# Two of four x1 tiles on VectorE, made between its scalings, and a copy on ScalarE that adds an immediate one

## The chip, the core and the metric

The kernel runs on one core of a Trainium2 chip. The time is the device time of one execution in microseconds (us). Five engines work beside one another: TensorE (PE: matmuls and transposes), VectorE (DVE), ScalarE (ACT), GpSimd (POOL: tensor operations and the issue of indirect DMAs) and SyncE (SP: DMA queues). They meet at semaphores only: an engine runs its own instructions in order, and an instruction in front of which a wait stands holds all that stands behind it on that engine.

## What is computed

Two graph layers over 50,000 nodes of 128 features and 12,500 edges, with a residual and a layer norm after each. Cut to what matters here:

```
# layer 0 (gnn), N = 50000, 128 channels
pooled = relu(layer_norm(x[src] * (1 + coeff * w) @ pool_w + pool_b))   # per edge
agg    = max(segment_max(pooled, dst), 0)
h      = relu(layer_norm([x, agg] @ final_w + final_b))
x1     = (x + h - mean) / sqrt(var + eps)                                # no gain, no bias
# layer 1 (RGCN, 8 bases), its own residual and norm
out    = norm(x1 + [agg_b(x1), x1] @ weight + bias)
```

## The kernel before

Rows of x are taken in groups of 512 (`CH = 4` tiles of 128 rows). There are 98 dense groups (`DENSE`), which are treated as if no edge ended in them, and 25 edge groups, which compute the rows anew that do have edges and scatter them over the others. The 98 tiles of edges go through the same steps, one a step, from step 8 (`LATE`) on. A stage with indirect gathers and the eight basis matmuls follows.

The whole first part is one software pipeline. `step(s)` is written out on each engine, and its pieces work on groups of different age. For VectorE a step (L986) below `EDGE_ORDER` = 104 is, in this order:

- moments and spread of the row statistics (L994, L995, L1000), and between them L1029: h = max(h, 0) + x for four tiles at once, behind a wait for GpSimd's addition `pool_b`;
- `variances` (L1005), which waits for sums of squares that ScalarE makes (`act_h`, `act_y`, `act_e`: the last of these is L755, for the edge tile), `stats_of(0)` (L1017), `inverses` (L1050, reciprocal), `stats_of(1)`;
- `scanned` (L1060), the segment maximum of an edge tile as a scan;
- `means` (L1068), which waits for ScalarE's square root (`act_q`, L720);
- `scaled`: `pooled` of the edge tile (L1074, reads the bank HE, signals `dve_te`), then four scalings of H by rows and gain into `hn` (L1078), the last of which signals `dve_t`;
- `stats_of(2)`, `stats_of(3)`, `dense_out` (L1089), and `first_layer` (L1110): the tiles of x1 from `X1_ACT` = 3 on, so one tile, as scalar_tensor_tensor with a second tensor input that is one column of `st` broadcast over 128; it signals `dve_x`.

In steps from 104 on `stats_of` stands ahead, `scaled` and `first_layer` behind one another, then `dense_out`.

ScalarE in a dense step: `turned` (L712, x1T = VT + 1, four tiles at once, as an Identity activation whose bias is the column `one`), `roots` (L720, square roots), `rooted` (L704, four squares of Y), `first_layer` (L744, x1 tiles 0 to 2), `squares` (L704, four squares of H; L755, square of HE behind a wait for `pe_e`), `rows_turned` (L765, copy of 640 columns).

TensorE in a dense step: transposes of x1 (L513, behind `act_x` and `dve_x`), root matmuls (L524), transposes of x (L537), H (L549, L551); then it waits for `dve_te` of the same step, that is for L1074, and for the scan. Behind that wait stand L567 and L568 (the pooled tile of the step before, turned), L573 and L574 (HE of the next tile, signals `pe_e`), and all of the next step.

GpSimd in a dense step: L436 (adds beta to the four tiles of `hn`, behind `dve_t`, signals `pool_b`), two indirect gathers (L406, L413), and L427 (scales gathered rows by a column).

Of the kernel before, what the change touches and what calls it, by code (L numbers as in the profile page):

```python
# [16 lines left out]
P = 128  # L17
CH = 4
# [53 lines left out]
def gnn_kernel(nc, x, src_cols, dst_cols, dst_next_cols, dst_rows, dst_prev_rows, type_line,  # L72
# [34 lines left out]
    with ExitStack() as ctx:  # L107
# [121 lines left out]
        W_TOP, W_POOL, W_BOT, W_ROOT, W_BASE = 0, 1, 2, 3, 4  # L229
        GAM_F, BET_F, GAM_P, BET_P = 3, 4, 5, 6  # L230
        N_CONST = 9
        X1_ACT = CH - 1

        def tiles_in(q):

# [22 lines left out]
        def is_group(c, k):  # L258

            return 0 <= c - k < GROUPS  # L260

        def is_dense(c, k):
            return 0 <= c - k < DENSE
# [9 lines left out]
        def x1_tile(g, m):  # L273

            return x1[:, g % 2, m, :] if g < DENSE else agg_all[:, (g - DENSE) * CH + m, :]
# [397 lines left out]
        def _(act):  # L673
# [25 lines left out]
            def step(s):  # L699
# [8 lines left out]
                def turned():  # L708
                    if is_group(c, 5):
                        act.wait_ge(S["pe_c"], s - 4)  # L710
                        need(act, S["pe_d"], s - 6)
                        nc.scalar.activation(x1T[:, 1 - b, :, :].rearrange("p c d -> p (c d)"), VT, ACT.Identity,  # L712
                                             bias=one[:, 0:1]).then_inc(S["act_c"], 1)

                def roots():
                    if 2 <= c <= GROUPS + 3:
# [103 lines left out]
        def _(dve):  # L820
# [187 lines left out]
            def step(s):  # L1008
# [10 lines left out]
                if stats:  # L1019
# [2 lines left out]
                        dve.wait_ge(S["dve_m"], min(s - 4, GROUPS))  # L1022
                    first = moments(RES, TOP, 1 - b)
                    read_at = own.count
                if fresh:
                    if is_dense(c, 3):
                        dve.wait_ge(S["pool_b"], s - 2)
                    h = hn[:, (c - 3) % SLOTS, :, :].rearrange("p c d -> p (c d)")
                    dve.scalar_tensor_tensor(h, h, 0.0, rows[:, (c - 3) % SLOTS, 0:CH, :].rearrange("p c d -> p (c d)"),  # L1029
                                             ALU.max, ALU.add).then_inc(S["dve_v"], 1)  # L1030
                if stats:
                    own.need(first)
                    spread_at = spread(RES, TOP)
# [34 lines left out]
                        dve.scalar_tensor_tensor(st[:, 3, TOP:TOP + CH], power[:, 1 - b, 0, RES:TOP], -0.5, st[:, 7, RES:TOP],  # L1068
                                                 ALU.mult, ALU.mult).then_inc(S["dve_m"], 1)

                def scaled():
                    if is_tile(c, 2):
                        need(dve, S["pe_cp"], s - LATE - 3)
                        dve.scalar_tensor_tensor(pooled[:, b, :], HE, st[:, 7, EDG:EDG + 1],  # L1074
                                                 vec_raw[:, GAM_P, :], ALU.mult, ALU.mult).then_inc(S["dve_te"], 1)
                    if is_group(c, 2):
                        for m in range(CH):
                            last = dve.scalar_tensor_tensor(hn[:, (c - 2) % SLOTS, m, :], H[b][:, cols(m, m + 1)],  # L1078
                                                            st[:, 7, TOP + m:TOP + m + 1], vec_raw[:, GAM_F, :],
                                                            ALU.mult, ALU.mult)  # L1080
                            if m < CH - 1:
                                own.mark(last)
                        last.then_inc(S["dve_t"], 1)

                def dense_out():
                    if is_dense(c, 7):
# [13 lines left out]
                def first_layer():  # L1100
                    if is_group(c, 4):
                        dve.wait_ge(S["dve_m"], s - 3)
                        if is_dense(c, 4):
                            need(dve, S["pe_c"], s - 5)
                        else:
                            dve.wait_ge(S["pe_b"], s - 3)
                        if is_dense(c, 4) and is_dense(c, 6):
                            dve.wait_ge(x1_stored[b], 16 * since(c, 4 + b, 2))
                        for m in range(X1_ACT, CH):
                            last = dve.scalar_tensor_tensor(x1_tile(c - 4, m), hn[:, (c - 4) % SLOTS, m, :],  # L1110
                                                            st[:, 7, RES + m:RES + m + 1],
                                                            st[:, 3, TOP + m:TOP + m + 1].broadcast_to([P, D]),
                                                            ALU.mult, ALU.add)
                            if m < CH - 1:
                                own.mark(last)
                        last.then_inc(S["dve_x"], 1)
# [6 lines left out]
                if c < EDGE_ORDER:  # L1123
                    at = variances()
                    residual_ready()
                    stats_of(0)
                    inverses(at)
                    stats_of(1)
                    scanned()
                    means()  # L1130
                    scaled()
                    stats_of(2)
                    stats_of(3)
                    dense_out()
                    first_layer()
                    edge_beta_added()
                else:
                    residual_ready()
                    stats_of(0)
                    at = variances()  # L1140
                    stats_of(1)
                    inverses(at)
                    stats_of(2)
                    stats_of(3)
                    scanned()
                    means()
                    scaled()
                    first_layer()
                    dense_out()
                    edge_beta_added()  # L1150
# [125 lines left out]
```

## Time and profile before

| | us |
|---|---|
| median of 3 runs | 920.42 (920.28 to 921.27) |
| the profiled execution, its span | 1001.7 |
| steps in order of the dense loop with edge tiles | about 65 to 520 of the span |
| edge groups | about 520 to 700 |
| gathers and bases | about 700 to 1001.7 |

The profiled execution is 81.3 us longer than the median. In all rows, times are us, "mean ns" excepted, and the idle time in brackets at the end of a timeline row is that of the engine before the row, with what ended it. Instructions of one engine overlap a little: one can start while the one ahead is still written out. So what an instruction costs its engine is the distance to the start of the next, and not its duration.

### The profile page before, as it was taken

What the parts mean: (1) busy time and instruction counts of PE and PEld (TensorE: products, weight loads), DVE (VectorE), ACT (ScalarE), POOL (GpSimd) and SP (SyncE); (2) the same over time, 40 slices, a digit from 0 to 9 for tenths busy, and PEclk for the clock granted to TensorE, in tenths of its full rate; (3) what the DMA queues carried; (4) which work ended last, traced back from release to release, by engine and by line L of the source; (5) the groups of instructions that cost most, each with busy time, mean ns of one, the idle gap of its engine ahead of it and who ended that gap; (6) DMA issues with size and microseconds to landing.
All of it is one profiled execution on the core that took longest, in us unless ns stands there. A gap on an engine that the chain in (4) does not pass through costs nothing. (4 is left out here: it accounts for less than half of the span.)

```text
span 1001.7 us, 18559 instructions
## 1 busy us (share of the span) xinstructions
PE 821.0 (82%) x4588; PEld 589.6 (59%) x4588; DVE 802.6 (80%) x2823; ACT 622.5 (62%) x2862; POOL 662.4 (66%) x702
## 2 busy tenths in 40 slices
PE   5889999999999999999997777674687887888790
PEld 3677777777777777777786666463343433443340
DVE  6989999999999999999997677553377774776891
ACT  4799999999999999999996555555001111111121
POOL 2667777777777777777756646466756666667544
PEclk9899999999999999999999898987789898888895
DMA  4466575655655556556552122241466676666640
GB/s 114 127 220 216 189 224 196 202 196 192 203 193 192 191 193 202 201 199 202 199 183 88 63 61 69 72 187 41 139 246 238 234 242 229 209 217 249 204 157 28
DMA packets 88575, 175.46 MB, mean 175 GB/s; under 512 B 16715, under 2 KB 34023, under 8 KB 82198
## 3 DMA queue, kind: packets, MB, share of 16 engines
q1 hardware_dynamic: 71286, 144.02, 42.5%
q0 software_dynamic: 15744, 29.71, 9.9%
q8 instruction: 38, 0.62, 0.3%
q10 hardware_dynamic: 1440, 0.56, 0.2%
q14 instruction: 67, 0.55, 0.2%
HBM read 105.88 MB, written 70.88 MB: 176 GB/s over the span
## 5 line engine op out<-in xcount | busy, mean ns | idle before, releaser
L704 ACT ACTIVATE junk<-ps 128x128 bf16<-128x128 f32 x884 | 234.8, 295 | 48.0 <-remote 18.1
L656 PE MATMUL ps<-agg_all,w_cen 128*128 128x512 f32 (+1 forms) x400 | 197.0, 648 | 38.9 <-DVE agg_all L1177 26.4
L704 ACT ACTIVATION_READ_ACCUMULATOR junk<-ps 128x1 f32 x884 | 196.6, 227 | 0.0
L436 POOL TENSOR_TENSOR work<-work,vec_raw 128x512 f32<-128x512 f32 x98 | 124.4, 1269 | 87.0 <-DVE work L1078 86.3
L551 PE MATMUL ps<-w_cen,xT 128*128 128x128 f32 x984 | 164.2, 300 | 0.0
L656 PEld LDWEIGHTS ps<-agg_all,w_cen 128*128 128x128 f32 x400 | 82.1, 211 | 138.0 <-issue 137.7
L806 ACT ACTIVATE st<-st 128x4 f32<-128x4 f32 x25 | 5.1, 206 | 235.2 <-issue 122.3
L551 PEld LDWEIGHTS ps<-w_cen,xT 128*128 128x128 f32 x984 | 133.3, 201 | 29.9 <-issue 29.9
L406 POOL DMA_INDIRECT x_table<-agg_all,scat_i x98 | 102.3, 1044 | 73.2 <-ACT agg_all L744 32.2
L1177 DVE TENSOR_TENSOR agg_all<-coefs,ps 128x1024 f32<-128x1024 f32 x98 | 117.4, 1209 | 39.4 <-PE ps L642 19.6
L524 PE MATMUL ps<-w_cen,work 128*128 128x128 f32 x984 | 137.0, 284 | 2.0 <-ACT y_root L730 1.5
L1078 DVE SCALAR_TENSOR_TENSOR work<-ps,st,vec_raw 128x128 f32<-128x128 f32 x492 | 137.2, 340 | 0.4 <-ACT st L720 0.3
L413 POOL DMA_INDIRECT rows<-x_table,src_i x98 | 93.7, 956 | 59.6 <-issue 30.2
L524 PEld LDWEIGHTS ps<-w_cen,work 128*128 128x128 f32 x984 | 126.6, 201 | 2.9 <-issue 2.9
L406 POOL DMA_INDIRECT x_dst<-in_x,dst_i x98 | 105.7, 1078 | 31.9 <-DMA x_dst_table<-x_dst 21.1
L406 POOL DMA_INDIRECT out_rows<-work,scat_i x98 | 97.5, 995 | 43.6 <-issue 29.2
L744 ACT ACTIVATE work<-work,st 128x128 f32<-128x128 f32 x294 | 125.6, 516 | 0.6 <-DVE st L1068 0.6
L1017 DVE BATCH_NORM_STATS2 bn<-work 128x6 f32<-128x128 f32 x492 | 123.0, 271 | 0.9 <-issue 0.3
L413 POOL DMA_INDIRECT rows<-in_x,src_i x98 | 94.9, 968 | 30.0 <-issue 29.3
L537 PE MATMUL ps<-ident,rows 128*128 128x128 f32 x590 | 90.6, 285 | 29.3 <-ACT xT L765 17.0
L712 ACT ACTIVATE work<-ps,one 128x512 f32<-128x512 f32 x123 | 91.7, 745 | 10.4 <-remote 10.0
L513 PE MATMUL ps<-ident,work 128*128 128x128 f32 x392 | 63.0, 284 | 36.2 <-issue 27.6
(139 smaller groups left out, 1445.8 us busy)
## 6 DMA issues: line engine op xcount, KB each, us to landing
coefs<-coef_line SPq DMA_DIRECT2D x49, 1024.0 KB
rows<-in_x SPq DMA_DIRECT2D x97, 256.0 KB
x_table<-work SPq DMA_DIRECT2D x97, 256.0 KB
out_rows<-outb SPq DMA_DIRECT2D x97, 256.0 KB
x_dst_table<-x_dst SPq DMA_DIRECT2D x98, 64.0 KB
rows<-x_dst_table SPq DMA_DIRECT2D x24, 256.0 KB
same_prev<-mask_line SPq DMA_DIRECT2D x7, 224.0 KB, 4.2
x_dst<-in_x,dst_i POOLq DMA_INDIRECT x98
```

The costliest lines, as they stand in the source:

```text
L406: return pool.indirect_dma_start(*args, bounds_check=last_node, oob_is_err=False)
L413: return pool.indirect_dma_start(rows_of, None, table, by(columns, t))
L436: pool.tensor_tensor(h, h, vec_raw[:, BET_F:BET_F + 1, :].broadcast_to([P, CH, D]), ALU.add).then_inc(S["pool_b"], 1)
L524: last = pe.matmul(Y[b][:, cols(m, m + 1)], x1T[:, b, m, :], w_cen[:, W_ROOT, :], start=True, stop=True, skip_group_check=True)
L551: last = pe.matmul(H[1 - b][:, cols(m, m + 1)], xT[:, 1 - b, m, :], w_cen[:, W_TOP, :], start=False, stop=is_dense(c, 1), skip_group_check ...
L656: last = pe.matmul(MT[b][:, 0:n * D], w_cen[:, W_BASE + m, :], prod[:, b, m, 0:n, :].rearrange("p t d -> p (t d)"), start=(m == 0), stop=( ...
L704: last = nc.scalar.activation(junk[:, kind * CH + m, :], bank[:, cols(m, m + 1)], ACT.Square, accum_out=power[:, b, 1, TOP + kind * CH + m ...
L712: nc.scalar.activation(x1T[:, 1 - b, :, :].rearrange("p c d -> p (c d)"), VT, ACT.Identity, bias=one[:, 0:1]).then_inc(S["act_c"], 1)
L744: last = nc.scalar.activation(x1_tile(c - 4, m), hn[:, (c - 4) % SLOTS, m, :], ACT.Identity, bias=st[:, 3, TOP + m:TOP + m + 1], scale=st[ ...
L1017: own.mark(dve.bn_stats(bn[:, RES + m, :], hn[:, (c - 3) % SLOTS, m, :]))
L1078: last = dve.scalar_tensor_tensor(hn[:, (c - 2) % SLOTS, m, :], H[b][:, cols(m, m + 1)], st[:, 7, TOP + m:TOP + m + 1], vec_raw[:, GAM_F, ...
L1177: dve.tensor_tensor(prod[:, b, half, two, :], coefs[:, p % COEF_SLOTS, :, half, :].rearrange("p t m d -> p m t d"), GX[c % len(GX)][:, col ...
```

## The change

ScalarE makes x1 tiles 0 and 1 and no longer 2. VectorE makes tiles 2 and 3, by tensor_scalar with two columns of scalars in place of scalar_tensor_tensor with a broadcast column. In dense steps these two stand between the third and the fourth scaling. The scan goes ahead of the second statistics, and `pooled` of the edge tile goes from ahead of the scalings to behind `stats_of(2)`. L712 becomes an addition of the immediate 1.0, without the column. In edge steps the order stays, only tiles and operations change.

```
-        X1_ACT = CH - 1
+        X1_ACT = 2
...
-                        nc.scalar.activation(x1T[:, 1 - b, :, :].rearrange("p c d -> p (c d)"), VT, ACT.Identity,
-                                             bias=one[:, 0:1]).then_inc(S["act_c"], 1)
+                        nc.scalar.add(x1T[:, 1 - b, :, :].rearrange("p c d -> p (c d)"), VT, 1.0).then_inc(S["act_c"], 1)
...
-                def scaled():
+                def pooled_scaled():
                     if is_tile(c, 2):
                         need(dve, S["pe_cp"], s - LATE - 3)
                         dve.scalar_tensor_tensor(pooled[:, b, :], HE, st[:, 7, EDG:EDG + 1],
                                                  vec_raw[:, GAM_P, :], ALU.mult, ALU.mult).then_inc(S["dve_te"], 1)
+
+                def scaled(tiles=range(CH)):
                     if is_group(c, 2):
-                        for m in range(CH):
+                        for m in tiles:
...
-                            last = dve.scalar_tensor_tensor(x1_tile(c - 4, m), hn[:, (c - 4) % SLOTS, m, :],
-                                                            st[:, 7, RES + m:RES + m + 1],
-                                                            st[:, 3, TOP + m:TOP + m + 1].broadcast_to([P, D]),
-                                                            ALU.mult, ALU.add)
+                            last = dve.tensor_scalar(x1_tile(c - 4, m), hn[:, (c - 4) % SLOTS, m, :],
+                                                     st[:, 7, RES + m:RES + m + 1],
+                                                     st[:, 3, TOP + m:TOP + m + 1], ALU.mult, ALU.add)
...
                     inverses(at)
+                    scanned()
                     stats_of(1)
-                    scanned()
                     means()
-                    scaled()
+                    scaled(range(3))
+                    first_layer()
+                    scaled(range(3, CH))
                     stats_of(2)
+                    pooled_scaled()
                     stats_of(3)
                     dense_out()
-                    first_layer()
                     edge_beta_added()
```

## Rows read from the trace of the kernel before

**Rows 1.** Busy time by stretch (columns: PE, PEld, DVE, ACT, POOL, clock, DMA)
```profile
300.00:400.00 100.00, 91.97 (x631) 72.69 (x630) 95.34 (x376) 95.46 (x477) 73.50 (x79) 1.00 0.60 196
```
**Rows 2.** Timeline of VectorE over one dense step (start, duration, instruction)
```profile
344.56 0.68 DVE L1029 SCALAR_TENSOR_TENSOR work<-work,rows 128x512 f32<-128x512 f32 x1
...
346.43 0.14 DVE L1068 SCALAR_TENSOR_TENSOR st<-power,st 128x4 f32<-128x4 f32 x1
346.49 0.34 DVE L1074 SCALAR_TENSOR_TENSOR pooled<-ps,st,vec_raw 128x128 f32<-128x128 f32 x1
346.75 1.11 DVE L1078 SCALAR_TENSOR_TENSOR work<-ps,st,vec_raw 128x128 f32<-128x128 f32 x4
347.78 0.47 DVE L1017 BATCH_NORM_STATS2 bn<-work 128x6 f32<-128x128 f32 x2
348.18 0.67 DVE L1089 TENSOR_TENSOR outb<-ps,st 128x512 f32<-128x512 f32 x1
348.77 0.59 DVE L1110 SCALAR_TENSOR_TENSOR work<-work,st 128x128 f32<-128x128 f32 x1
349.28 0.15 DVE L994 TENSOR_TENSOR st<-bn 128x4 f32<-128x4 f32 x1
```
**Rows 3.** Timeline of all engines around another dense step
```profile
352.87 0.23 PE L567 MATMUL ps<-ones,edge_beta 3*128 3x128 bf16 x1
352.88 1.27 POOL L436 TENSOR_TENSOR work<-work,vec_raw 128x512 f32<-128x512 f32 x1 [0.74 <-DVE work L1078]
...
353.60 0.49 PE L574 MATMUL ps<-w_cen,xT 128*128 128x128 f32 x2
...
353.71 0.59 DVE L1110 SCALAR_TENSOR_TENSOR work<-work,st 128x128 f32<-128x128 f32 x1
...
354.47 1.49 POOL L406 DMA_INDIRECT x_dst<-in_x,dst_i  x1 [0.32 <-DMA x_dst_table<-x_dst]
...
357.27 0.41 POOL L427 TENSOR_TENSOR rows<-rows,e_scale 128x128 f32<-128x128 f32 x1
```
**Rows 4.** L1110 by itself, dense (100 to 500) and edge steps (560 to 620)
```profile
L1110 DVE SCALAR_TENSOR_TENSOR work<-work,st x80: 584/593/1240, 101.1 to 498.3; 128x128 f32<-128x128 f32 x80
```
```profile
L1110 DVE SCALAR_TENSOR_TENSOR agg_all<-work,st x9: 341/341/344, 561.2 to 617.3; 128x128 f32<-128x128 f32 x9
```
**Rows 5.** Timeline of ScalarE, from one release by TensorE to its next step
```profile
336.50 0.28 ACT L704 ACTIVATE junk<-ps 128x128 bf16<-128x128 f32 x1 [1.02 <-PE ps L524]
```
```profile
341.22 0.30 ACT L704 ACTIVATE junk<-ps 128x128 bf16<-128x128 f32 x1
```
**Rows 6.** Timeline of ScalarE, from the square of HE to the next copies
```profile
56.78 0.36 ACT L755 ACTIVATE junk<-ps 128x128 bf16<-128x128 f32 x1
...
57.03 0.79 ACT L765 COPY xT<-ps 128x640 f32<-128x640 f32 x1
...
57.60 0.80 ACT L712 ACTIVATE work<-ps,one 128x512 f32<-128x512 f32 x1
```
**Rows 7.** Timeline of an edge step where each engine waits for the one before
```profile
544.08 0.59 ACT L730 COPY y_root<-ps 128x512 f32<-128x512 f32 x1 [1.97 <-remote]
544.56 0.22 ACT L720 ACTIVATE st<-st 128x13 f32<-128x13 f32 x1
544.81 0.17 DVE L1068 SCALAR_TENSOR_TENSOR st<-power,st 128x4 f32<-128x4 f32 x1 [1.96 <-ACT st L720]
544.89 0.35 DVE L1074 SCALAR_TENSOR_TENSOR pooled<-ps,st,vec_raw 128x128 f32<-128x128 f32 x1
...
545.29 0.09 PEld L567 LDWEIGHTS ps<-ones,edge_beta 3*128 3x128 bf16 x1 [2.65 <-DVE pooled L1074]
```
**Rows 8.** Timeline: a tensor_scalar of VectorE within an indirect DMA's issue
```profile
585.01 0.98 POOL L406 DMA_INDIRECT x_table<-agg_all,scat_i  x1 [5.98 <-ACT agg_all L744]
...
585.36 0.23 DVE L929 TENSOR_SCALAR agg_now<-agg_now 98x128 f32<-98x128 f32 x1
...
586.29 0.98 POOL L406 DMA_INDIRECT x_table<-agg_all,scat_i  x1 [0.30 <-issue]
```

More of the change, by code:

```diff
@@ L1024, in step, with residual @@
                     read_at = own.count
[L1025 to L1030, printed above, removed]
+                def residual():
+                    if fresh:
+                        if is_dense(c, 3):
+                            dve.wait_ge(S["pool_b"], s - 2)
+                        h = hn[:, (c - 3) % SLOTS, :, :].rearrange("p c d -> p (c d)")
+                        dve.scalar_tensor_tensor(h, h, 0.0,
+                                                 rows[:, (c - 3) % SLOTS, 0:CH, :].rearrange("p c d -> p (c d)"),
+                                                 ALU.max, ALU.add).then_inc(S["dve_v"], 1)
+                residual()
                 if stats:
@@ L1082, in scaled @@
                                 own.mark(last)
-                        last.then_inc(S["dve_t"], 1)
+                            else:
+                                last.then_inc(S["dve_t"], 1)
                 def dense_out():
@@ L1146, in step @@
                     means()
+                    pooled_scaled()
                     scaled()
```

## The prediction

> **What bounds the kernel now.** I read the busy time by stretch first, which finds the long even part and its clock, then the timelines of one step, engine by engine, and last the same instruction in two stretches. In the dense stretch TensorE, VectorE and ScalarE are busy for 92, 95 and 95 of 100 us, at full granted clock [rows 1]. No engine has room by itself, so the order within a step decides. L1110 stands once in each dense step, 80 times from 101.1 to 498.3 [rows 4], so a step takes 397.2 / 79 = 5.03 us on average. An undisturbed one takes 353.71 - 348.77 = 4.94 [rows 2, 3]: in it VectorE starts one instruction close behind the other from L1029 to L994, and no wait for a semaphore shows [rows 2]. The rest, 0.09 a step, are stalls of ScalarE of up to a microsecond (rows 5, the first, is one), which reach VectorE later.
>
> One instruction of VectorE is longer than its work. L1110 takes 0.59 in dense steps and 0.34 in edge steps [rows 4]. In the dense step it runs while GpSimd adds beta: L436 ends at 352.88 + 1.27 = 354.15 and L1110 at 354.30 [rows 3]. In edge steps there is no L436. So some 0.25 us of each dense step is VectorE held by GpSimd. Without it VectorE's step would be 4.69. ScalarE by itself needs 341.22 - 336.50 = 4.72 for a step that it goes through without a long wait [rows 5]. These are the two near ties of today.
>
> **The change, part by part.**
>
> *L1110 goes from the end of the step.* It holds VectorE for 349.28 - 348.77 = 0.51 [rows 2]. That is removed.
>
> *Two tensor_scalar come in.* The trace has none of this form with two columns of scalars. Nearest is L929, 98x128 with immediates, 0.23 long [rows 8]; instructions of that length give way to the next some 0.08 early, as L1074 does (0.34 long, next start after 0.26 [rows 2]), so 0.15. The statistics L1017, one input and no scalar column, give way after (348.18 - 347.78) / 2 = 0.20; the scalings L1078, with one scalar column, after (347.78 - 346.75) / 4 = 0.26 [rows 2]. So a scalar column costs about 0.06 (an estimate, as L1078 also has a second tensor). The bounds for one tensor_scalar, called t, are 0.15 (the columns are free) and 0.20 + 2 x 0.06 = 0.32. L929 with one or two columns gives 0.21 or 0.27. I take t = 0.22, nearest to L929 with one column paid in full, and two of them 0.44. VectorE's own step is then 4.94 - 0.51 + 0.44 = 4.87, 0.07 less than now.
>
> L929 is the one row of this operation, and it is shorter than L1017 though it has a similar size. The Trainium skill, VectorE: DVE Perf Modes, "Mode 2×_2P", says that a one-input fp32 operation from SBUF to SBUF moves two elements a cycle; it agrees with L929. By its table of costs (58 cycles and one for two elements at 0.96 GHz) t would be an estimated 0.13, and VectorE's step 4.69.
>
> *ScalarE loses one of three L744 and the bias column.* A tile of L744 holds it for at least the 57.03 - 56.78 = 0.25 that the square of one tile takes [rows 6]; L712 to L720 becomes what a copy of the same size without a column takes, 544.56 - 544.08 = 0.48 [rows 7], a tenth less. ScalarE's own step falls from 4.72 to 4.37 or less. It is no bound any more, and part of the 0.09 a step from its stalls should be absorbed; I leave 0.05 (an estimate: half).
>
> *`pooled` (L1074) is moved behind three scalings, two x1 tiles, a fourth scaling and one statistics.* This is the part that costs. TensorE waits for it in the same step, ahead of L567, and L567, L568, L573, L574 and the whole next step are queued behind that wait. Now L1074 ends 0.40 after L1068 starts [rows 2], and L567 shows no idle time ahead of it [rows 3]: nobody waits. After the change it ends 0.06 + 3 x 0.26 + 2t + 0.26 + 0.20 + 0.34 = 1.63 + 2t after L1068 starts [rows 2]. A closed loop of one step hangs on it: L1074, then TensorE 0.05 later (544.89 + 0.35 to 545.29 [rows 7]), L567 to the end of L574 in 354.09 - 352.87 = 1.22 [rows 3], ScalarE another 0.05 later (an estimate, as the last hop), L755 0.25, L765 0.57 [rows 6], L712 0.48 [rows 7], then L720, to L1068 of the next step 0.25 [rows 7]. ScalarE's order allows nothing else: L720 stands behind L765 and L712. Sum: 1.63 + 0.05 + 1.22 + 0.05 + 0.25 + 0.57 + 0.48 + 0.25 = 4.50, plus 2t = 4.94. Today the same loop has 0.40 in place of 1.63 + 2t and some 0.10 more for L712: 3.4, with 1.5 us to spare. All of that is spent.
>
> *The fourth scaling is later, so GpSimd's L436 is.* It starts 0.08 behind the scaling's end, at 1.17 + 2t + 0.08 after L1068, ends at 2.52 + 2t, then L1029 may go, and from L1029 to L1068 it is 346.43 - 344.56 = 1.87 [rows 2]: 4.39 + 2t, some 0.05 more for the hop: 4.88. Just below the loop above.
>
> *The scan ahead of the second statistics:* the same two instructions stand between L1050 and L1068, nothing. *TensorE* gets x1 earlier, but with 92 of 100 us busy [rows 1] its own step is about 4.6: nothing either way. *Edge steps* (25): VectorE has one tile more (2t - 0.26 = 0.18), ScalarE one less; both tiles are needed, and GpSimd issues a scatter every 586.29 - 585.01 = 1.28 [rows 8], four to a group, 5.1 a step, which hides that. If that cover went, 25 x 0.18 = 4.5 us. Behind 700 nothing is changed.
>
> **Sum.** The longest of the loops is 4.94, with 0.05 for stalls 4.99, against 5.03. About 90 dense steps have all parts (455 us from 65 to 520, by 5.03): 90 x -0.04 = -3.6 us in the profiled execution, from 1001.7 to 998.1. That execution is 81.3 longer than the median, and where isn't shown; I take the same difference: 920.4 - 3.6 = 916.8.
>
> **The rivals.**
>
> *Cheap tiles.* If t is 0.15, the loop is 4.80 and the average 4.85: -0.18 x 90 = -16, 904. For it: L929. Against: two scalar columns, of which none is seen to be free. With the 0.13 of the Trainium skill, VectorE: DVE Perf Modes, it would be an estimated 901.
>
> *GpSimd gets in the way of the x1 tiles (slower).* L1110 shows that VectorE is held when it reads through what GpSimd holds. The two tensor_scalar stand from 0.83 to 1.27 after L1068. In rows 3 L427 starts 357.27 - 352.88 = 4.39 after L436, behind a gather that was late and long (L406, 1.49). With that distance it would start at 1.69 + 4.39 - 4.94 = 1.14 after L1068, on the second tile. L1029 will now start right behind L436 and so ahead of L406, and may make L406 long each time. If L427 falls on the tiles in most steps, they wait up to its 0.41, and this lies on the loop in full. It decides from the point where L427 starts later than 0.42 after L1068, 0.41 ahead of the tiles. A mean of 0.2 a step, with t = 0.22 to 0.27, with the 0.05 of stalls gives 5.19 to 5.29, and +14 to +23: 935 to 944. Against: GpSimd is idle for 0.74 ahead of L436 [rows 3], and the tiles stand in that gap in a step where it is punctual.
>
> *The tile isn't cheaper than today's.* If t is 0.26, what L1078 takes, the loop is 5.02 and the average 5.07: +3.6, 924.
>
> *Issue of the DMAs suffers.* In edge steps a tensor_scalar would fall into scatters. The rows speak against it: L929 ran inside one, which took 0.98 like the next [rows 8]. If each of 50 held the queue for its 0.22, that is +11 on the forecast: 928. The Trainium skill, SBUF — State Buffer, "Who interferes with whom", has this rule: VectorE in a two-port mode and GpSimd shut each other out, writing of descriptors included; by it the time would be the same 928, in edge steps, and the trace doesn't agree for L929.
>
> **How the numbers follow.** Forecast 0.41 (911 to 923, of which faster 0.23, same 0.12, slower 0.06), cheap tiles 0.22 (901 to 911), GpSimd in the way 0.23 (926 to 944), tile not cheaper 0.09 (same 0.03, slower 0.06), DMA issue 0.05. Faster by over 0.2% 0.45, within 0.2% (about what a measurement of this kernel can tell) 0.15, slower 0.40. The range, 902 to 939, leaves out the ends of the first and second rival.
>
> **What would show it.** Right: in dense steps TensorE's load for L567 idle, released by L1074; VectorE's L1068 idle, released by L720, which starts at once behind L712; ScalarE idle ahead of L755; steps of 4.9 to 5.0. L1110's 0.59 gone. Wrong: tensor_scalar rows of 0.4 and more that end with a GpSimd row; no wait at L567; L1029 waiting for L436 by more than 0.1; a changed pace between 520 and 700. The number is wrong by 1.8 us for each 0.01 in t.

## The result, and the profile after

| | kernel before | changed kernel |
|---|---|---|
| device time, median | 920.85 us | 940.75 us (940.13 to 941.15) |
| ratio | 1 | 1.0207, 95% interval 1.0186 to 1.0228 |
| span of a profiled execution | 916.4 us | 939.2 us |

The change makes the kernel 2.1% slower. Forecast was 916.8, in a range of 902 to 939.

Executions come in two kinds: beside some runs the kernel before takes about 920 us, beside others 985 to 1003, called the 920 kind and the 1000 kind from here on. The profile behind the prediction (span 1001.7) is of the second kind. The profile of before in the table above is another execution (`before_3` below), of the first kind, like the profile of the changed kernel. So all comparisons of totals below are made within one kind. Whether the kind belongs to the chip isn't shown: runs of both kinds carry chip number 0.

First, the busy time by stretch, as in [rows 1] (PE, PEld, DVE, ACT, POOL, clock, DMA). The changed kernel:

```profile
300.00:400.00 100.00, 87.04 (x622) 71.15 (x623) 96.19 (x388) 85.19 (x441) 81.41 (x78) 1.00 0.58 192
```

The kernel before, in an execution of the same kind (before_3):

```profile
300.00:400.00 100.00, 93.70 (x650) 74.83 (x649) 97.24 (x385) 98.73 (x491) 75.30 (x82) 1.00 0.60 199
```

The granted clock is 1.00 in both, the upper of its two levels. TensorE and ScalarE are busy for 7 and 14 us less in 100 (ScalarE also has one x1 tile less to make in each step). The list of waits of the changed kernel from 100 to 500 (us in total, times, longest) names for whom they wait:

```profile
PEld ps L567 <- DVE pooled L1078: 67.6, 77, 1.3
ACT junk L754 <- PE ps L574: 58.7, 77, 1.0
PE ps L567 <- DVE pooled L1078: 53.1, 77, 1.1
POOL work L436 <- DVE work L1084: 39.0, 77, 1.0
```

Once in each of 77 steps TensorE waits 0.88 us for the moved `pooled` (now L1078; lines behind the change are shifted, L1068 is L1072 and L755 is L754), and ScalarE waits 0.76 for TensorE. Those are two of the links of the prediction's closed loop. Its rows, from one step of the timeline of all engines:

```profile
353.89 0.16 DVE L1072 SCALAR_TENSOR_TENSOR st<-power,st 128x4 f32<-128x4 f32 x1
...
353.97 0.86 DVE L1084 SCALAR_TENSOR_TENSOR work<-ps,st,vec_raw 128x128 f32<-128x128 f32 x3
...
354.75 0.68 DVE L1117 TENSOR_SCALAR work<-work,st 128x128 f32<-128x128 f32 x2
354.82 0.51 POOL L427 TENSOR_TENSOR rows<-rows,e_scale 128x128 f32<-128x128 f32 x1
355.35 0.34 DVE L1084 SCALAR_TENSOR_TENSOR work<-ps,st,vec_raw 128x128 f32<-128x128 f32 x1
...
355.61 0.28 DVE L1016 BATCH_NORM_STATS2 bn<-work 128x6 f32<-128x128 f32 x1
...
355.76 1.26 POOL L436 TENSOR_TENSOR work<-work,vec_raw 128x512 f32<-128x512 f32 x1 [0.43 <-DVE work L1084]
355.81 0.33 DVE L1078 SCALAR_TENSOR_TENSOR pooled<-ps,st,vec_raw 128x128 f32<-128x128 f32 x1
...
356.19 0.09 PEld L567 LDWEIGHTS ps<-ones,edge_beta 3*128 3x128 bf16 x1 [0.83 <-DVE pooled L1078]
...
356.92 0.49 PE L574 MATMUL ps<-w_cen,xT 128*128 128x128 f32 x2
...
357.06 0.69 DVE L1030 SCALAR_TENSOR_TENSOR work<-work,rows 128x512 f32<-128x512 f32 x1
...
357.17 1.49 POOL L406 DMA_INDIRECT x_dst<-in_x,dst_i  x1
...
357.45 0.28 ACT L754 ACTIVATE junk<-ps 128x128 bf16<-128x128 f32 x1 [0.72 <-PE ps L574]
...
357.71 0.69 ACT L764 COPY xT<-ps 128x640 f32<-128x640 f32 x1
...
358.29 0.61 ACT L712 ACTIVATE work<-ps 128x512 f32<-128x512 f32 x1
...
358.78 0.22 ACT L719 ACTIVATE st<-st 128x13 f32<-128x13 f32 x1
...
359.03 0.17 DVE L1072 SCALAR_TENSOR_TENSOR st<-power,st 128x4 f32<-128x4 f32 x1
```

From start to start along the loop: L1072 0.08, three scalings 0.78, two tiles 0.60, fourth scaling 0.26, statistics 0.20, then 355.81 to 356.19 for L1078 and the hop, 1.26 to the release of L754 at 357.45, then 0.26, 0.58, 0.49 and 0.25. Sum 5.14, which is 359.03 - 353.89, and the median step of this kernel. The last link, from ScalarE's root L719 to VectorE's L1072, makes a wait too short for the list: L719 ends at 359.00 and L1072 starts at 359.03, and in the median L1072 comes 0.25 behind the start of the statistics ahead of it, where it comes 0.18 behind when the root is early (wait_moved below). The same rows in the kernel before, L1068 to L1068 of VectorE:

```profile
302.82 0.14 DVE L1068 SCALAR_TENSOR_TENSOR st<-power,st 128x4 f32<-128x4 f32 x1
...
307.72 0.14 DVE L1068 SCALAR_TENSOR_TENSOR st<-power,st 128x4 f32<-128x4 f32 x1
```

4.90. A step is read from here on as the distance between two of these instructions. Where the time of the whole went is a sum over three stretches, in us. The dense stretch goes from the start of this instruction in step 10 to its start in step 104; the edge stretch follows, and then the rest:

| kernel | kind | median step, 100 to 500 | mean of 94 steps | dense | edge | rest | span |
|---|---|---|---|---|---|---|---|
| before, first profile | 1000 | 4.92 | 5.055 | 475.1 | 157.1 | 310.9 | 1001.7 |
| before_3 | 920 | 4.91 | 4.958 | 466.0 | 122.5 | 271.0 | 916.4 |
| changed | 920 | 5.14 | 5.211 | 489.8 | 119.4 | 271.5 | 939.2 |

Of the 22.8 us between the two spans on the 920 kind, the dense steps take +23.8, the edge stretch -3.1, the rest and the start +0.5 and +1.6. The two kinds have the same median step for the kernel before; they differ in single long steps, and above all in the edge stretch and behind it. Median steps are therefore compared across kinds below, totals aren't.

### The profile page after: what moved, and what is told of

The parts are those of the page before. It is cut to its first block and busy times, and to the rows that moved or that the text cites. A ratio compares the mean times of both kernels' runs of the same rounds, so it can differ in the third digit from the quotient of the medians.

```text
span 939.2 us, 18559 instructions
## 1 busy us (share of the span) xinstructions
PE 769.8 (82%) x4588; PEld 566.3 (60%) x4588; DVE 824.2 (88%) x2946; ACT 569.3 (61%) x2739; POOL 706.3 (75%) x702
## 5 line engine op out<-in xcount | busy, mean ns | idle before, releaser
L656 PE MATMUL ps<-agg_all,w_cen 128*128 128x512 f32 (+1 forms) x400 | 177.7, 598 | 2.0 <-DVE agg_all L1186 1.2
L436 POOL TENSOR_TENSOR work<-work,vec_raw 128x512 f32<-128x512 f32 x98 | 124.0, 1265 | 71.6 <-DVE work L1084 71.3
L406 POOL DMA_INDIRECT x_dst<-in_x,dst_i x98 | 143.9, 1469 | 15.7 <-DMA x_dst_table<-x_dst 1.7
L1084 DVE SCALAR_TENSOR_TENSOR work<-ps,st,vec_raw 128x128 f32<-128x128 f32 x492 | 145.8, 342 | 0.4 <-ACT st L719 0.3
L1016 DVE BATCH_NORM_STATS2 bn<-work 128x6 f32<-128x128 f32 x492 | 133.9, 277 | 0.9 <-DVE st L1004 0.3
L524 PE MATMUL ps<-w_cen,work 128*128 128x128 f32 x984 | 132.0, 278 | 0.5 <-DVE outb L1096 0.5
L406 POOL DMA_INDIRECT x_table<-agg_all,scat_i x98 | 101.2, 1033 | 40.2 <-issue 26.6
L656 PEld LDWEIGHTS ps<-agg_all,w_cen 128*128 128x128 f32 x400 | 76.2, 196 | 87.3 <-issue 86.9
L524 PEld LDWEIGHTS ps<-w_cen,work 128*128 128x128 f32 x984 | 121.5, 194 | 1.0 <-issue 1.0
L406 POOL DMA_INDIRECT out_rows<-work,scat_i x98 | 97.4, 994 | 29.8 <-issue 28.6
L413 POOL DMA_INDIRECT rows<-in_x,src_i x98 | 95.0, 969 | 29.9 <-issue 29.6
L413 POOL DMA_INDIRECT rows<-x_table,src_i x98 | 93.5, 954 | 31.8 <-issue 28.6
L743 ACT ACTIVATE work<-work,st 128x128 f32<-128x128 f32 x196 | 89.1, 527 | 0.6 <-DVE st L1072 0.6
L1030 DVE SCALAR_TENSOR_TENSOR work<-work,rows 128x512 f32<-128x512 f32 x123 | 84.9, 690 | 0.0
L537 PEld LDWEIGHTS ps<-ident,rows 128*128 128x128 f32 x590 | 69.9, 145 | 22.9 <-ACT xT L764 11.8
```

Source lines behind the costliest of these rows:

```text
L406: return pool.indirect_dma_start(*args, bounds_check=last_node, oob_is_err=False)
L413: return pool.indirect_dma_start(rows_of, None, table, by(columns, t))
L436: pool.tensor_tensor(h, h, vec_raw[:, BET_F:BET_F + 1, :].broadcast_to([P, CH, D]), ALU.add).then_inc(S["pool_b"], 1)
L524: last = pe.matmul(Y[b][:, cols(m, m + 1)], x1T[:, b, m, :], w_cen[:, W_ROOT, :], start=True, stop=True, skip_group_check=True)
L537: last = pe.transpose(XT[:, cols(m, m + 1)], rows[:, slot, m, :], ident[:, :])
L656: last = pe.matmul(MT[b][:, 0:n * D], w_cen[:, W_BASE + m, :], prod[:, b, m, 0:n, :].rearrange("p t d -> p (t d)"), start=(m == 0), stop=( ...
```

## The experiments

Each ratio is to the kernel before timed beside it, so within one kind. Line numbers are those of the run's own kernel.

**pooled_first: the changed kernel with `pooled` ahead of the scalings again.** This takes the loop through L1078 away and leaves the tiles.

```diff
                     means()
+                    pooled_scaled()
                     scaled(range(3))
                     first_layer()
                     scaled(range(3, CH))
                     stats_of(2)
-                    pooled_scaled()
                     stats_of(3)
```

> The changed kernel, with pooled of the edge tile back ahead of the scalings; all else as changed. Theory A (two loops of a step: one by TensorE, ScalarE and back to VectorE through pooled, 5.14 us; one by GpSimd's beta addition, from the fourth scaling over L436 to the residual L1030, 5.03): the first falls to under 4.2, but the fourth scaling comes 0.26 later, so the second rises to 5.2 or 5.3: 944 to 956, slower than the change, with no wait of TensorE for pooled and a wait of VectorE ahead of L1030. Theory B (only the wait of TensorE for pooled costs): VectorE's own work decides, 4.94 to 5.03 a step, 921 to 931. Theory C (the tensor_scalars or the meeting with L427 cost, wherever pooled stands): as the change, 938 to 943.

953.24 against 921.54, ratio 1.0329 (1.0306 to 1.0353); median step 5.29. Timeline of that kernel, GpSimd and VectorE:

```profile
303.51 1.27 POOL L436 TENSOR_TENSOR work<-work,vec_raw 128x512 f32<-128x512 f32 x1 [0.69 <-DVE work L1084]
...
304.34 0.46 DVE L993 TENSOR_TENSOR st<-bn 128x4 f32<-128x4 f32 x1
...
304.81 0.69 DVE L1030 SCALAR_TENSOR_TENSOR work<-work,rows 128x512 f32<-128x512 f32 x1
```

L436 ends at 304.78 and L1030 starts at 304.81. The second loop of the prediction (fourth scaling, L436, L1030 and back) now carries the step: with `pooled` back in front it is some 0.25 longer (5.29, against 5.04 below). The place of `pooled` was right. Two loops lie close together, and shortening one is worth only the distance to the next.

**wait_moved: the changed kernel, TensorE waits for `pooled` only ahead of L573 and L574.** In the code HE (written by L573 and L574) and the output of L567 and L568 lie in one bank of PSUM, so a wait for ScalarE's read of HE stands ahead of L567 in this kernel, and `pooled` waits for L568 of its own step.

```diff
                 if is_tile(c, 2):
-                    pe.wait_ge(S["dve_te"], s - LATE - 1)
...
                     pe.wait_ge(S["dve_te"], s - LATE - 2)
+                    pe.wait_ge(S["act_e"], min(s - LATE - 1, TILES))
...
+                if is_tile(c, 2):
+                    pe.wait_ge(S["dve_te"], s - LATE - 1)
                 if is_tile(c, 1):
                     if c == LATE + 1:
...
-                        need(dve, S["pe_cp"], s - LATE - 3)
+                        need(dve, S["pe_cp"], s - LATE - 2)
```

> The changed kernel, where TensorE does L567 and L568 (pooled of the step before, turned) ahead of its wait for pooled of this step; the wait stands in front of L573. pooled waits for L568, and L567 for ScalarE's last square, since they share a bank. Theory A: the first loop loses the 0.58 of L567 and L568; the next longest are TensorE's own chain with pooled in it, 4.99, and GpSimd's, 5.03: 928 to 934. Theory B: VectorE's own work, 4.94 to 5.03, 921 to 931. Theory C: unchanged, 938 to 943.

937.24 against 921.54, ratio 1.0163 (1.0144 to 1.0182), above the 928 to 934 expected; median step 5.04. Timeline (L573 is now L574):

```profile
302.07 1.26 POOL L436 TENSOR_TENSOR work<-work,vec_raw 128x512 f32<-128x512 f32 x1 [0.43 <-DVE work L1085]
...
302.50 0.09 PEld L574 LDWEIGHTS ps<-pool_bias,ones 3*128 3x128 bf16 x1 [0.69 <-DVE pooled L1079]
...
303.37 0.69 DVE L1031 SCALAR_TENSOR_TENSOR work<-work,rows 128x512 f32<-128x512 f32 x1
...
304.84 0.21 ACT L720 ACTIVATE st<-st 128x13 f32<-128x13 f32 x1 [0.21 <-DVE st L1055]
```

The loop through `pooled` is open now: ScalarE stands idle for 0.21 ahead of its root L720 and waits for VectorE, which in the changed kernel it doesn't. The median step became 5.14 - 5.04 = 0.10 shorter, the 94 dense steps 9.8 us, and they stop at GpSimd's loop: L1031 starts 0.04 after L436 ends. The total improved less, as the edge stretch took 126.4 in place of 119.4; why wasn't tried. So with the loop through `pooled` opened, the changed kernel is still slower than before.

**pooled_late and one_tile: half of the change each.** pooled_late is the kernel before with `pooled` moved behind `scaled` and `stats_of(2)`, with all its tiles as they were:

```diff
                     means()
                     scaled()
                     stats_of(2)
+                    pooled_scaled()
                     stats_of(3)
                     dense_out()
                     first_layer()
```

one_tile is the changed kernel with three tiles on ScalarE:

```diff
-        X1_ACT = 2
+        X1_ACT = 3
```

> The kernel before, with one edit alone: in dense steps pooled of the edge tile goes behind the four scalings and the third statistics. Theory A: the loop through pooled is 4.61 without x1 tiles in it, under the others; the last scaling comes 0.26 earlier, L436 too, and L1110 isn't held any more (0.34 in place of 0.59), so VectorE needs 4.69 and ScalarE 4.72 a step: 900 to 905. Theory B (pooled behind the scalings costs by itself): 921 or more. If the hold of L1110 is hidden anyway: 919 to 922.

> The changed kernel with X1_ACT = 3: ScalarE makes three x1 tiles as before, VectorE one, by tensor_scalar between the third and the fourth scaling. Theory A: both loops lose a tile of 0.26 to 0.30: 4.84 to 4.88 and 4.73; ScalarE's own step 4.62: 911 to 917. If ScalarE with three tiles is the bound (it was near it before): 920 or more. If the tile isn't on the path: unchanged, 938 to 943.

pooled_late: 906.72 against 921.54, ratio 0.9823 (0.9789 to 0.9857), step 4.74. one_tile: 911.87, ratio 0.9893 (0.9877 to 0.991), step 4.80. Both are faster than before. pooled_late was expected at 900 to 905 and misses that by 1.7. The window of pooled_late, and rows of its VectorE and GpSimd:

```profile
300.00:400.00 100.00, 96.76 (x679) 78.00 (x678) 96.94 (x403) 100.00 (x507) 77.48 (x85) 1.00 0.63 209
```

```profile
301.33 0.16 DVE L1068 SCALAR_TENSOR_TENSOR st<-power,st 128x4 f32<-128x4 f32 x1
...
302.62 1.26 POOL L436 TENSOR_TENSOR work<-work,vec_raw 128x512 f32<-128x512 f32 x1 [0.58 <-DVE work L1080]
...
303.69 0.34 DVE L1112 SCALAR_TENSOR_TENSOR work<-work,st 128x128 f32<-128x128 f32 x1
...
306.08 0.16 DVE L1068 SCALAR_TENSOR_TENSOR st<-power,st 128x4 f32<-128x4 f32 x1
```

The tile of VectorE takes 0.34 and not 0.59. The scalings end earlier by the 0.26 of `pooled`, GpSimd's L436 runs earlier, and the tile (here L1112) starts only 0.19 ahead of its end, where it was 0.44 [rows 3]. It still ends 0.15 behind L436, as in [rows 3], but 0.15 behind is now also where an unheld tile would end. ScalarE is busy for all of the 100 us: the step of 4.74 is ScalarE's own, the 4.72 of the prediction [rows 5]. With the new order and one tile the step is 4.80, which is the loop's 4.54 and one tile of 0.26; with the second tile, 5.14. So it is the second tile that costs, 0.34 a step.

**one_ts_at_end, two_at_end, add_only: the parts in the old order.** one_ts_at_end is the kernel before with a `tensor_scalar` at L1110; two_at_end has two of them there (`X1_ACT = 2`); add_only has the copy with the immediate alone.

```diff
-                            last = dve.scalar_tensor_tensor(x1_tile(c - 4, m), hn[:, (c - 4) % SLOTS, m, :],
-                                                            st[:, 7, RES + m:RES + m + 1],
-                                                            st[:, 3, TOP + m:TOP + m + 1].broadcast_to([P, D]),
-                                                            ALU.mult, ALU.add)
+                            last = dve.tensor_scalar(x1_tile(c - 4, m), hn[:, (c - 4) % SLOTS, m, :],
+                                                     st[:, 7, RES + m:RES + m + 1],
+                                                     st[:, 3, TOP + m:TOP + m + 1], ALU.mult, ALU.add)
```

> The kernel before, with its one tile L1110 as tensor_scalar at the old place at the end of the step, in the time of L436. If one tensor input escapes the hold by GpSimd: 0.34 in place of 0.59, VectorE's step 4.69, ScalarE's 4.72 bounds: 901 to 906. If it is held just the same: 0.59, 4.94 a step, 919 to 922.

> The kernel before with X1_ACT = 2 and tensor_scalar, both tiles at the old place at the end of the step, pooled ahead of the scalings: the second tile moved from ScalarE to VectorE and nothing reordered. Theory A (VectorE's own order and L436 bound the step): 4.94 less 0.06 for the shorter hold, and 0.26 for the second tile: 5.14 to 5.20 a step, +16 to +22 us on the kernel before, so the reordering neither costs nor brings much beside it. Theory B (the second tile is harmless and the reordering costs): 4.90 to 5.00, 0 to +2.

> The kernel before with L712 alone changed to the addition of an immediate. ScalarE's own step goes from 4.72 to 4.62, while VectorE holds the step at 4.94: 0 to -3 us on the kernel before. If ScalarE was the bound: 0.10 x 94 = -9.

one_ts_at_end: 995.25 against 1003.38, ratio 0.9936 (0.99 to 0.9972), step 4.88. two_at_end: 1002.92 against 995.31, ratio 1.0062 (1.0017 to 1.0107), step 5.08. add_only: 994.95, ratio 0.9981 (0.9939 to 1.0023), step 4.91, as before: the copy alone brings nothing, since ScalarE isn't what holds the step there. The timeline of one_ts_at_end:

```profile
303.18 1.27 POOL L436 TENSOR_TENSOR work<-work,vec_raw 128x512 f32<-128x512 f32 x1 [1.55 <-DVE work L1078]
...
304.00 0.53 DVE L1110 TENSOR_SCALAR work<-work,st 128x128 f32<-128x128 f32 x1
...
304.45 0.15 DVE L994 TENSOR_TENSOR st<-bn 128x4 f32<-128x4 f32 x1
```

L1110 ends 0.08 behind L436, at 304.53; the old form ended 0.15 behind it in [rows 3]. With one tensor input it is held nearly as long as with two: the form doesn't free it, and the step is 0.03 shorter. two_at_end was overpriced: its total was expected 16 to 22 above, and is 7.6 above. Its median step is 5.08, under the 5.14 to 5.20 expected and 0.17 longer than before; in the mean of 94 steps it is 0.11 longer (5.140 against 5.028 in before_again), as the kernel before has more long steps.

**two_tensors and no_columns: the price of the tile itself.** two_tensors is the changed kernel with its two tiles in the old form. no_columns is the changed kernel with immediates (1.0 and 0.5) in place of the two columns of scalars, so it leaves out the normalisation of two of the four x1 tiles. The edit of no_columns:

```diff
-                            last = dve.tensor_scalar(x1_tile(c - 4, m), hn[:, (c - 4) % SLOTS, m, :],
-                                                     st[:, 7, RES + m:RES + m + 1],
-                                                     st[:, 3, TOP + m:TOP + m + 1], ALU.mult, ALU.add)
+                            last = dve.tensor_scalar(x1_tile(c - 4, m), hn[:, (c - 4) % SLOTS, m, :],
+                                                     1.0, 0.5, ALU.mult, ALU.add)
```

> The changed kernel, with its two x1 tiles of VectorE made by scalar_tensor_tensor with the broadcast column, as before, at the place between the third and the fourth scaling. Theory A1 (a tile costs 0.26 in either form, and GpSimd's L427 gets in the way of either): 5.14 to 5.16 a step, 938 to 943. Theory A2 (the one-input form is worth its name): with two inputs each tile is held to the end of L427, 0.1 to 0.3 a step more: 950 to 968.

> The changed kernel with immediates 1.0 and 0.5 in place of the two scalar columns of both tensor_scalars, so two of four x1 tiles aren't normalised. It measures what the columns cost. Two tiles with columns hold VectorE for 0.51 in edge steps of the changed kernel. If a column costs 0.06: two tiles in 0.26 there, the dense step 4.89 to 4.95, 917 to 923. If the two columns together cost 0.06: 0.38, 5.02, 929. If columns are free: no change, 938 to 943.

two_tensors: 1016.59 against 1003.38, ratio 1.0162 (1.0105 to 1.022), step 5.22. no_columns: 1004.23, ratio 1.0028 (0.9985 to 1.0071), step 5.04, not the 4.89 to 4.95 expected if a column costs 0.06. In edge steps no GpSimd arithmetic is beside the tiles, so their own price is read there. The changed kernel's VectorE:

```profile
566.64 0.59 DVE L1117 TENSOR_SCALAR agg_all<-work,st 128x128 f32<-128x128 f32 x2
567.15 0.69 DVE L1104 TENSOR_TENSOR work<-work,vec_raw 128x512 f32<-128x512 f32 x1
```

no_columns:

```profile
564.21 0.35 DVE L1117 TENSOR_SCALAR agg_all<-work 128x128 f32<-128x128 f32 x2
564.48 0.68 DVE L1104 TENSOR_TENSOR work<-work,vec_raw 128x512 f32<-128x512 f32 x1
```

Two tiles take 0.51 with columns and 0.27 without: 0.255 and 0.135 each, so 0.12 for the two columns of a tile, 0.06 for each if they cost alike (no run has one column alone). In the dense step of two_tensors:

```profile
304.80 0.75 DVE L1117 SCALAR_TENSOR_TENSOR work<-work,st 128x128 f32<-128x128 f32 x2
304.87 0.53 POOL L427 TENSOR_TENSOR rows<-rows,e_scale 128x128 f32<-128x128 f32 x1
305.47 0.34 DVE L1084 SCALAR_TENSOR_TENSOR work<-ps,st,vec_raw 128x128 f32<-128x128 f32 x1
```

0.67 from the tiles to the next scaling, 0.07 more than in the changed kernel, and the median step is 0.07 longer too (5.215 against 5.144). One tensor input saves only in the meeting with L427, not alone (0.255 against the 0.26 of the old form in edge steps of before, where L1110 is 0.34 long [rows 4]). The dense step of no_columns:

```profile
304.78 0.58 DVE L1117 TENSOR_SCALAR work<-work 128x128 f32<-128x128 f32 x2
304.85 0.41 POOL L427 TENSOR_TENSOR rows<-rows,e_scale 128x128 f32<-128x128 f32 x1
305.27 0.34 DVE L1084 SCALAR_TENSOR_TENSOR work<-ps,st,vec_raw 128x128 f32<-128x128 f32 x1
```

The tiles that take 0.27 alone take 0.49 here, to the end of L427 at 305.26. The loop is then 4.54 + 0.49 = 5.03, and the step 5.04. Tiles half as dear give back 0.10 a step, 5.14 - 5.04, and not the 0.24 that they save when they run alone, since L427 holds them for the rest.

**tiles_earlier: the tiles behind the first scaling instead of the third.**

```diff
                     means()
-                    scaled(range(3))
+                    scaled(range(1))
                     first_layer()
-                    scaled(range(3, CH))
+                    scaled(range(1, CH))
                     stats_of(2)
```

> The changed kernel, with the two x1 tiles behind the first scaling and no longer behind the third, so 0.52 earlier and ahead of GpSimd's L427, beside its gather L413. Both loops keep the same work. Theory A (0.09 of the 0.60 that two tiles take in a dense step is the meeting with L427): 0.51 for two, 5.05 a step, 930 to 934. If an indirect DMA's issue holds a tensor_scalar as well: 0.3 a step more, 955 to 970. If the 0.60 has another cause: 938 to 943.

1013.21 against 1003.38, ratio 1.0132 (1.0075 to 1.0189), step 5.15: no gain, against what was expected. Its timeline:

```profile
301.09 0.96 POOL L413 DMA_INDIRECT rows<-in_x,src_i  x1 [0.30 <-issue]
...
301.49 0.69 DVE L1117 TENSOR_SCALAR work<-work,st 128x128 f32<-128x128 f32 x2
...
302.07 0.42 POOL L427 TENSOR_TENSOR rows<-rows,e_scale 128x128 f32<-128x128 f32 x1
302.11 0.85 DVE L1084 SCALAR_TENSOR_TENSOR work<-ps,st,vec_raw 128x128 f32<-128x128 f32 x3
```

L427 starts only 302.07 - 301.49 = 0.58 after the tiles' start now, and they still take 0.62, beside the issue of the gather L413. What they left behind they met again ahead.

**pooled_late_add, and repeats.** pooled_late with the copy by an immediate as well. ScalarE is the bound of pooled_late, and this gives it the 0.1 of the column back:

```diff
-                        nc.scalar.activation(x1T[:, 1 - b, :, :].rearrange("p c d -> p (c d)"), VT, ACT.Identity,
-                                             bias=one[:, 0:1]).then_inc(S["act_c"], 1)
+                        nc.scalar.add(x1T[:, 1 - b, :, :].rearrange("p c d -> p (c d)"), VT, 1.0).then_inc(S["act_c"], 1)
```

> The kernel before with pooled behind the third statistics and the immediate addition. pooled_late alone left ScalarE busy without a gap at 4.74 a step; now ScalarE needs 4.62 to 4.64 and VectorE 4.69: 4.68 to 4.72 a step, 3 to 6 us less than pooled_late, so -17 to -22 on the kernel before. If TensorE's wait for pooled or its own work is the bound: as pooled_late, -13 to -16.

> The kernel of pooled_late_add again. If its 0.9 us waits of ScalarE at the squares of Y come from its own order (ScalarE's step of 4.62 is shorter than VectorE's, so it comes early to each wait): 5.05 to 5.2 a dense step again, whatever the chip. If from the chip of that call: 4.70 to 4.80 on another.

> The kernel of pooled_late again, beside pooled_late_add on one chip. In its first run it had no wait of ScalarE at its squares of Y and 4.81 a dense step (steps 10 to 104). If that belongs to the kernel: 4.76 to 4.85 again, 12 to 20 us under the kernel before of this call. If it belonged to the chip of that call: 5.0 to 5.15 and squares of Y that wait 0.9 us in many steps, -2 to +8.

> The changed kernel again, on the chip of the two others: 5.19 to 5.23 a dense step from step 10 to 104, no wait at the squares of Y, 12 to 21 us over the kernel before of this call. If the loss belonged to its first chip: within 5 of it.

> The kernel before, for a profile on a chip where it takes about 920. If only the edge stretch and the rest are shorter there: dense steps of 4.95 to 5.03 (steps 10 to 104), edge about 120, rest about 272. The sum of the prediction took 5.03 and the same dense steps for both. If the dense step is at the undisturbed 4.92 there, the stalls were worth nothing in the timed runs and the forecast began 8 us off.

The first time, in the 1000 kind, 1002.07 against 995.31, ratio 1.0077 (1.0029 to 1.0126): a clear miss. Its list of waits, 100 to 500:

```profile
DVE st L1004 <- ACT junk L754: 35.3, 35, 1.4
ACT junk L704 <- PE ps L524: 29.4, 34, 1.0
```

ScalarE stands still for 0.86 us 34 times ahead of the squares of Y. The same kernel in the 920 kind (pooled_late_add_2) has no such row, takes 906.11 against 920.11, ratio 0.9825 (0.9784 to 0.9866), with a median step of 4.65. The mean of its 94 dense steps is 4.835, above the 4.813 and 4.820 of the two runs of pooled_late: the median step fell by 0.09 and the sum of the steps didn't, as 18 of its steps are over 0.4 longer than the median, against 9 and 12. pooled_late again gives 906.81, ratio 0.9851 (0.9834 to 0.9867), the changed kernel 940.23, ratio 1.023 (1.0213 to 1.0247), and before_3, a single execution of the kernel before, 918.24 against another single one of 923.63. In the 1000 kind a single execution of the kernel before (before_again) gave 985.6 against 995.31, with an edge stretch of 148.7 and a rest of 303.8.

> The kernel before once more, for a profile on the chip of this call. Dense steps from step 10 to 104 took 5.055 us each in its first profile, whose span was 1001.7. If the 81 us between span and median lie behind the dense steps, they take 4.98 to 5.06 here as well, with the edge stretch at about 120 and the rest at 272 in place of 157 and 311. If they lie in the dense steps: under 4.5.

The long waits of ScalarE put down to L524 are seen in the 1000 kind alone, and how many there are changes with the kernel: 14 and 9 in the two profiles of before, 14 in add_only, 19 in one_ts_at_end, 27 in two_at_end, 34 in pooled_late_add, and none in two_tensors, no_columns and tiles_earlier, which have the changed kernel's order or one close to it. So their number goes with both, the kind and the kernel. pooled_late and pooled_late_add are 1.5 to 1.8% faster than the kernel before where that takes 920; between the two no difference is seen there. In the 1000 kind only pooled_late_add was run, and it lost. The changed kernel itself was timed in the 920 kind alone.

## Why the prediction was wrong

**Right: what bounds the step.** The loop through L567, L574 and ScalarE is the bound. Its waits at L567 and at L754 are in the list, and the third, at L1072, is the 0.25 - 0.18 = 0.07 read above, less than the list shows. Its constant part was predicted 4.50 and is 5.14 - 0.60 = 4.54. The loop through L436 was predicted at 4.39 + 2t + 0.05; with 2t = 0.60 that is 5.04, and wait_moved, where it alone is left, has a step of 5.04. ScalarE's own 4.72 holds (pooled_late, 4.74). The copy brings nothing by itself (add_only). ScalarE's lighter load wasn't tried without the second tile on VectorE.

**Wrong, first: the term 2t.** I took t = 0.22, "nearest to L929 with one column paid in full". Both columns are paid, 0.12 on top of 0.135: two tiles alone take 0.51, not 0.44. The sum of my own bounds, 0.15 plus two columns of 0.06, gives 0.27; there was no row for a free column, and I leaned that way. That is +0.07 a step. The rival of cheap tiles was no way out either: no_columns has them at 0.135, and is at 1.0028 of before instead of 2% faster. "Wrong by 1.8 us for each 0.01 in t" failed with it: t fell by 0.12, and the median step by 0.10, some 9 us in 94 steps and not 22, by the meeting with L427.

**Wrong, second: GpSimd in the way of the tiles was a rival and not in the sum.** It came as that rival has it, step by step. L1030 starts 0.11 ahead of L406 (357.06 and 357.17) and L406 takes 1.49 in the median of all dense steps, where before L406 went first and took 1.04. So the gather L413 and behind it L427 come 0.45 later: L427 starts 354.82 - 353.89 = 0.93 after L1072, past the 0.42 from which the rival decides, and on the first tile. The meeting costs 0.60 - 0.51 = 0.09 in the median step and not the 0.2 of its price: the tile started first, and L427 took a part of the delay (0.51 for 0.41). That L406 is what brings L427 onto the tiles is read from the order in the trace; it wasn't changed by itself. What was taken for its contrary, GpSimd's idle 0.74 ahead of L436 [rows 3], was a gap of the old order. The forecast's loop of 4.94 becomes 4.94 + 0.04 + 0.07 + 0.09 = 5.14.

**Wrong, third: what the sum was compared with.** 4.99 was set against 5.03, the mean of a profile of the 1000 kind, and the difference taken off the median of 920.4. In the 920 kind a step of before is 4.958 in the mean of 94 steps, since the stalls of ScalarE that I meant to absorb are mostly absent. I had written that the 81.3 us between that profile and the median couldn't be placed, and then took the dense step as unaffected. Against 4.958 the same loop of 4.99 already is slower: 94 x 0.03 = +3 us instead of -3.6.

Together: the mean step is 5.211, 0.22 above 4.99, 94 x 0.22 = 21; the baseline adds 94 x 0.07 = 7; the edge stretch gives 3 back, which was predicted as 0. 916.8 + 21 + 7 - 3 = 942, against 940.75. The forecast's own sign for a wrong term, "tensor_scalar rows of 0.4 and more that end with a GpSimd row", is there: the second tile of a pair takes 0.42 in the median and ends 0.09 behind L427.

The change of a step with the parts of the change (median step; the first two runs are of the 1000 kind):

| kernel | step | against before |
|---|---|---|
| before | 4.91 | |
| one tensor_scalar at the end (one_ts_at_end) | 4.88 | -0.03 |
| two at the end (two_at_end) | 5.08 | +0.17 |
| `pooled` late alone (pooled_late) | 4.74 | -0.17 |
| new order, one tile (one_tile) | 4.80 | -0.11 |
| new order, two tiles (changed) | 5.14 | +0.23 |

The prediction never priced the order without the second tile. The early scalings are worth 0.17, since L436 ends before it can hold L1110 for long; putting two tiles between them gives that back and more.

Open: what the 0.86 us waits of ScalarE are. The profile puts them down to L524, and in the code L524's semaphore is the only one waited for there, but in pooled_late_add L524 had ended 1.1 to 1.2 us before ScalarE went on, in 33 of the 34 cases. So no engine's work that the profile shows ends them. Open is also what makes the two kinds of executions. Open too are the edge stretch of wait_moved and the long steps of pooled_late_add_2.

## What to carry to other kernels

When work is moved from an engine with room to one that has none, price the new position as well as the instruction: sum each closed loop that passes through it, and check what the shift does to the other engines' places. Undo a bundled change in halves; here one part (`pooled` late, the rest as before) was worth 1.5 to 1.8% where the kernel before takes 920, and the second tile took more than that. Take the baseline of a sum from a profile whose span agrees with the time it is compared with, and use medians of single steps where it doesn't.

## What the runs showed of the hardware

Two columns of scalars cost VectorE 0.12 us on a 128x128 tile: 0.135 with two immediates (no_columns), 0.255 with two columns (the changed kernel), both in edge steps. The Trainium skill, VectorE: DVE Perf Modes, "Mode 2×_2P", gives two elements a cycle for this form, and by the page's table of costs a tile would take an estimated 0.127; no_columns agrees. With columns next to nothing of that advantage is left when the tile runs alone: 0.255 against 0.26 for the two-tensor form in two_tensors.

The opening has the engines meet at semaphores only. The rows show that they also hold one another without one. A pair of `tensor_scalar` or a single one that GpSimd's work reaches into is held: by L436 (0.53 for 0.34), by L427 (two in 0.60 for 0.51, in 0.49 for 0.27 without columns), and beside the issue of the gather L413 (two in 0.62 for 0.51). In one_tile the tile starts 0.06 ahead of L427:

```profile
304.85 0.34 DVE L1117 TENSOR_SCALAR work<-work,st 128x128 f32<-128x128 f32 x1
304.91 0.52 POOL L427 TENSOR_TENSOR rows<-rows,e_scale 128x128 f32<-128x128 f32 x1
```

It isn't held, and L427 is (0.52 for 0.41). The Trainium skill, SBUF — State Buffer, "Who interferes with whom", says that VectorE in a two-port mode and GpSimd shut each other out of a shared pair of ports, and that the one that issues first keeps it for its whole instruction. These rows agree, and L929 in [rows 8] doesn't.

How long an indirect DMA's issue takes beside a 128x512 operation of two SBUF inputs goes with which of the two starts first. In pooled_late L406 starts at 304.03, L1029 at 304.15:

```profile
304.03 1.04 POOL L406 DMA_INDIRECT x_dst<-in_x,dst_i  x1
...
304.15 0.68 DVE L1029 SCALAR_TENSOR_TENSOR work<-work,rows 128x512 f32<-128x512 f32 x1
```

In the changed kernel L1030 starts 0.11 ahead in the median, and L406 takes 1.49 to 1.50 in all of its 77 dense steps from 100 to 500. In the three profiles of before and in pooled_late L406 starts first in 251 dense steps of that stretch, and takes 1.03 to 1.05 in each. A tenth of a microsecond in who comes first goes with 0.45 on all that follows on GpSimd.
